# Layer 2 of a two-layer transformer kernel: GpSimd's powers, masks, gathers and folds in another order

## The chip, the cores and the metric

The kernel runs on one core of a Trainium2 chip. The metric is the device time of one execution in microseconds (us), and the time of a kernel is the median over several runs.

## The reference, cut to what matters

The program computes two layers on an input of 8 batches with 512 tokens of 128 features. Layer 1 is windowed attention plus a top-1 mixture of eight experts; it is not touched here. Layer 2 is causal attention with 16 heads of 64 (one key and one value head for all of them, normalised queries and keys) plus a gated feed-forward part. This is the core of layer 2 for one batch:

```python
xn = layernorm(x, g1)
q = xn @ Wq.T                          # 16 heads of 64
kv = xn @ Wkv.T                        # one k and one v, 64 wide
q, k = l2norm(q * 16), l2norm(k)       # each row divided by its length
sim = einsum('bhid,bjd->bhij', 4 * q, 4 * k)
sim = where(causal_mask, -max, sim)
attn = softmax(sim)
out = layernorm(einsum('bhij,bjd->bhid', attn, v) @ Wout.T, g2)
x = x + out + w_down(silu(gate) * up)
```

## The kernel before, in words

Five engines run programs of their own and meet at semaphores. Everything is written out by hand: the order of the lines in an engine's function is the order in which that engine issues them, and an instruction that waits holds up all that stands behind it on its engine.

Layer 2 (phase C, with the preparation of the next batch, R, woven into it) is a loop over the 8 batches. Seven of them run as a hardware loop with `last=False`, the eighth apart with `last=True`, without the work for a next batch. Within a batch, `attend` loops on every engine over n = 0 to 7. Each n is one **pair** of heads.

- TensorE (`pe`), at n: `scores(n)` in three parts ("thirds") into PSUM, `project_q(n + 2)`, `turn_q(n + 1)` (transposes), `gate_up` for small n, then `values1(n - 1)`, the product of masked probabilities and v. `project_q(n + 2)` needs the bank that `q_unit(n + 1)` on VectorE reads. `scores(n)` needs `q_lo` of pair n for its last matmuls.
- ScalarE (`act`), at n: the exponentials of the three thirds, the squares of the next projected q, and the copies of the turned q.
- VectorE (`dve`), at n: `q_sums` (sums of squares), `q_low(n + 1)`, `values_out(n - 1)` (the copy at L2056), then `q_unit(n + 2)`: `inverse` waits for GpSimd's power, clips it (TENSOR_SCALAR, L1958), takes the reciprocal (L1960), and L2011 scales the queries. At n = 3 it adds the experts' rows of the next batch, which GpSimd has gathered; at n = 4 it takes that batch's row statistics; at n = 5 and 6 it normalises and, in `add_blocks`, adds up the probability blocks of pairs 4 and 5.
- GpSimd (`pool`), at n: `q_length(n + 1)` raises the sums to the power 0.5 (TENSOR_TENSOR, L1272), four AFFINE_SELECTs mask pair n (L1313), and there are three rarer pieces. `fetch` issues indirect DMAs (L1231), one for each of four tiles, that gather the experts' rows of the next batch; `both_roots` computes two inverse roots for that batch's norms (L1098 to L1101); `fold(k)` issues an accumulating DMA (L1293, 384 KB) that adds the second key block's probabilities of pair k to those of the first. It is done for pairs 0 to 3 (`N_FOLD = 4`), and it waits until `values1(k)` has read them.

The folded blocks save TensorE matmuls in `sums1(m)`, which forms the softmax denominators of pairs 2m and 2m + 1. `sums1(0)` stands in TensorE's program at the end of n = 5, `sums1(1)` at n = 6 between `scores(6)` and `turn_q(7)`.

In the text, "the power k" is `q_length(s, k, b)`, and "the masks of n" are the four selects of pair n. The power k is issued at n = k - 1 and feeds `q_unit(k + 1)`, which TensorE awaits at `project_q(k + 2)`, or at `turn_q(7)` for k = 6.

Of the kernel before, what the change touches and what calls it, by code (L numbers as in the profile page):

```python
# [16 lines left out]
ALU = mybir.AluOpType  # L17
# [46 lines left out]
N_FOLD = 4  # L64
# [34 lines left out]
PER_C = dict(squared=6, q_full=6, q_free=6, o_full=7, o_free=7, l_full=1, l_free=1, s_full=15, s_free=15, m_full=8, m_free=8, w_full=11, w_free=11,  # L99
             e_full=10, e_free=9, own=17, var=1, veps=1, rstd=1,  # L100
             sums=6, lens=6, q_lo=8, h1=3, masked=24, pv=4, added4=6, g_free=2, inverted=1, fin=1, stored=16,
             folded=16 * N_FOLD)

CREDITED = dict(q_lo=1, q_free=1, o_free=1, l_free=1, s_free=1, m_free=1, w_free=1, e_free=1, g_free=1, sums=1, h1=1, r_free=1, added=1, stored=1, pv=1,
                xt_free=1, y_full=1, y_free=1, staged=2, out0=1, out1=1, out2=1, out3=1)
# [148 lines left out]
def two_layers(nc, x, wq, bq, wk, bk, wv, bv, wo, bo, w_router, w1, b1, w2, b2,  # L254
# [4 lines left out]
    with ExitStack() as ctx:  # L259
# [104 lines left out]
        def probs_of(n, j):  # L364

            at, many, step, skip = ((1536, 512, 512, 0), (512, 384, 512, 0), (0, 256, 256, 0), (512, 128, 512, 384))[j]
            return probs1[n % PB][:, at:at + 2 * step].rearrange("p (c t) -> p c t", c=2)[:, :, skip:skip + many]
# [100 lines left out]
        def apart(eng):  # L468

            eng.sem_inc(s_apart[0 if eng is nc.vector else 1], 1)  # L470
# [21 lines left out]
        def _(pe):  # L492
            pe.wait_ge(s_pool, N_IDENT)

            def mm(out, lhs, rhs, start=True, stop=True):
                return pe.matmul(out, lhs, rhs, start=start, stop=stop, skip_group_check=True)  # L496
# [188 lines left out]
            s = SB  # L685
# [103 lines left out]
            def attend(b, last):  # L789
                s = SC  # L790
# [65 lines left out]
                def p_of(n, c, j):  # L856
                    at, many = ((1536, 512), (512, 384), (0, 256), (896, 128))[j]
                    at += c * (256 if j == 2 else 512)
                    return probs1[n % PB][:, at:at + many]
# [10 lines left out]
                def sums1(m):  # L870

                    if m == 0:
                        pe.wait_ge(s["g_free"].sem, s["g_free"].at(b, 0))
                    if m < N_FOLD // 2:
                        pe.wait_ge(s["folded"].sem, s["folded"].at(b, 32 * (m + 1)))
                    if m == 2:
                        pe.wait_ge(s["added4"].sem, s["added4"].at(b, 6))
                    for j in ((0, 2, 3), (0, 2, 3), (0,), range(NT))[m]:
                        for h in range(HG):
                            ins = mm(gather[32 * h:32 * h + 32, j * P:T], pick_sum[:, m, :], p_of(2 * m + h // 2, h % 2, j),  # L880
                                     start=(m == 0 and j == 0), stop=(m == NP // 2 - 1 and j == NT - 1))
                    ins.then_inc(s["pv"].sem, s["pv"].add(1))
# [177 lines left out]
        def _(pool):  # L1060
# [32 lines left out]
            def both_roots(b):  # L1093

                s = SR
                pool.wait_ge(s["var"].sem, s["var"].at(b, 1))
                apart(pool)
                pool.tensor_scalar(veps2[:, 0, :], mv[:, :, 1], EPS, None, ALU.add).then_inc(s["veps"].sem, s["veps"].add(1))  # L1098
                pool.tensor_scalar(veps2[:, 1, :], mv[:, :, 1], 1.0 + EPS, EPS * EPS, ALU.mult, ALU.add).then_inc(s["veps"].sem, s["veps"].add(1))
                pool.wait_ge(s["veps"].sem, s["veps"].at(b, 2))  # L1100
                pool.tensor_tensor(rstd2[:].rearrange("p a i -> p (a i)"), veps2[:].rearrange("p a i -> p (a i)"),  # L1101
                                   exponents[:, 0:2 * NT], ALU.pow).then_inc(s["rstd"].sem, s["rstd"].add(1))
# [27 lines left out]
            def attend(b):  # L1130

                for n in range(FINISH if now.kind == "finish" else SLOTS):
                    if n % HG == MASK_LAG % HG and (now.own if n >= MASK_LAG else now.past):
                        mask((n - MASK_LAG) % SLOTS // HG)
                    if n == AT_ADD_BIAS and now.own:
                        if now.kind == "first":
                            pool.wait_ge(s_early, 32)
                        add_bias(b)
                    if n == AT_ROOT and now.own and now.ahead:
                        x_root()  # L1140
# [31 lines left out]
            assert n_late[0] == N_LATE  # L1172
            now.open("first", 0)
            attend(0)
            for b in range(1, B - 1):
                now.open("loop", b)
                attend(b)
# [37 lines left out]
            def fetch_slots(b, behind=True):  # L1215

                s = SR
                s["picked"].restart()
                s["back"].restart()
                if behind:  # L1220
                    pool.wait_ge(s["added"].sem, s["added"].at(b, 0))
                apart(pool)
                pool.tensor_copy(slots_now[:], slots[:, bass.ds(b * NT, NT)]).then_inc(s["picked"].sem, s["picked"].add(1))

            def fetch(b, tiles_of):

                s = SR
                pool.wait_ge(s["picked"].sem, s["picked"].at(b, 1))
                apart(pool)
                for i in tiles_of:  # L1230
                    pool.indirect_dma_start(y_back[:, i, :], None, slots_y[0:(TT + NE - 1) * P], bass.IndirectOffsetOnAxis(  # L1231
                        ap=slots_now[:, i:i + 1], axis=0)).then_inc(s["back"].sem, s["back"].add(16))
# [35 lines left out]
            def q_length(s, k, b):  # L1268

                pool.wait_ge(s["sums"].sem, s["sums"].at(b, k))  # L1270
                half = half_of(s, k - 1 if s is SR else k)
                pool.tensor_tensor(q_len[:, half], q_sum[:, half], exponents[:, 2 * NT:4 * NT],  # L1272
                                   ALU.pow).then_inc(s["lens"].sem, s["lens"].add(1))

            def k_length(b):
                s = SR
                pool.wait_ge(s["sums"].sem, s["sums"].at(b, 1))
                pool.tensor_tensor(klen[:], ksum[:], exponents[:, 2 * NT:3 * NT], ALU.pow).then_inc(s["lens"].sem, s["lens"].add(1))

            def attend(b, last):  # L1280
                s = SC
                for name in ("veps", "rstd", "lens", "masked"):
                    s[name].restart()
                for name in () if last else ("veps", "rstd", "lens"):
                    SR[name].restart()

                def fold(n):

                    pool.wait_ge(s["o_full"].sem, s["O"].filled(b, ("o", n)))
                    if n:  # L1290
                        pool.wait_ge(s["folded"].sem, s["folded"].at(b, 16 * n))
                    apart(pool)
                    pool.dma_start(probs_of(n, 0)[:, :, P:T], probs_of(n, 1),  # L1293
                                   accum_op=ALU.add).then_inc(s["folded"].sem, s["folded"].add(16))

                s["folded"].restart()
                for n in range(NP):
                    if 0 <= n - 2 < N_FOLD:
                        fold(n - 2)
                    if n + 2 < NP:  # L1300
                        q_length(s, n + 1, b)
                    p = probs1[n % PB]
                    for third in (0, 1, 2):
                        ring = (s["M"], s["S"], s["W"])[third]
                        pool.wait_ge(ring.free.sem, ring.emptied(b, ("probs", n, third)))
                        apart(pool)
                        if third == 0:
                            diagonals = [p[:, 512:1536].rearrange("p (c t) -> p c t", c=2)[:, :, at:at + P] for at in (0, 384)]
                        else:
                            at, many = (None, (0, 512), (1536, 1024))[third]  # L1310
                            diagonals = [p[:, at:at + many].rearrange("p (c t) -> p c t", c=2)[:, :, 0:P]]
                        for v in diagonals:
                            ins = pool.affine_select(out=v, in_=v, compare_op=ALU.is_ge, fill=0.0, base=0,  # L1313
                                                     pattern=[[0, 2], [1, P]], channel_multiplier=-1)
                        ins.then_inc(s["masked"].sem, s["masked"].add(1))
                    if not last and n == 0:
                        fetch_slots(b + 1)
                    if not last and n in (1, 2):
                        fetch(b + 1, (2 * n - 2, 2 * n - 1))
                    if not last and n == 4:  # L1320
                        both_roots(b + 1)
                if not last:
                    k_length(b + 1)
                    q_length(SR, 2, b + 1)
                    q_length(SR, 3, b + 1)
                root(s, 1, b)
# [878 lines left out]
```

## Time and profile before

| | |
|---|---|
| time, median of 3 runs | 1240.59 us (1240.56 to 1241.66) |
| the profiled execution's own time | 1239.02 us |
| its span, first to last instruction | 1237.2 us |
| layer 2 in it | from about 610 us on; 77.0 us for a batch |
| TensorE matmuls busy | 1145.6 us, 93% of the span |
| VectorE busy | 921.7 us, 74% |
| GpSimd busy | 490.6 us, 40% |

The shares are means over the whole program. Within layer 2 the seven batches of the loop look nearly the same, so the rows below are mostly of one of them, whose n = 0 begins at about 1005 us.

### The profile page before, as it was taken

The numbers are of one execution on the slowest core, as the hardware profiler recorded it, in microseconds if no ns is written. First come the engines' busy times: TensorE is split into PE (matmuls) and PEld (weight loads), VectorE is DVE, ScalarE is ACT, GpSimd is POOL, SyncE is SP. The second block draws the span as 40 slices with busy tenths as digits, with TensorE's granted clock in tenths as the row PEclk, the third lists the DMA queues.
The fourth block names the chain that finished last, engine by engine and source line by source line (L and its number), as shares of the span: only waits on it lengthen the run. The fifth ranks groups of instructions, "written<-read, shape, count | busy, mean of one in ns | idle before, by whom it ended". The sixth has DMA issues, their size and how long they took to land.

```text
span 1237.2 us, 26393 instructions
## 1 busy us (share of the span) xinstructions
PE 1145.6 (93%) x8475; PEld 782.4 (63%) x8475; DVE 921.7 (74%) x2473; ACT 672.3 (54%) x1290; POOL 490.6 (40%) x691
## 2 busy tenths in 40 slices
PE   5999999999999998899399999999999999999996
PEld 3656666666666554799265857657576575765764
DVE  7888888888888897455456868668686686866755
ACT  2767676666676755355173552735527355273550
POOL 5122212121222311554364481744817448274450
PEclk8999999999999998899799999999999999999999
DMA  3311212020101000122011030210302103021020
GB/s 89 101 44 48 56 28 57 26 60 26 33 18 27 18 18 1 44 64 55 15 35 27 9 59 0 42 25 8 59 0 42 25 8 59 0 49 19 15 46 10
DMA packets 43718, 42.31 MB, mean 34 GB/s; under 512 B 7040, under 2 KB 36224, under 8 KB 43648
## 3 DMA queue, kind: packets, MB, share of 16 engines
q0 software_dynamic: 11008, 17.31, 8.0%
q1 hardware_dynamic: 32640, 24.15, 7.3%
q8 instruction: 34, 0.56, 0.2%
q14 instruction: 36, 0.29, 0.1%
HBM read 13.72 MB, written 6.75 MB: 17 GB/s over the span
## 4 chain that ended last, share of the span: by engine, by line
issue 19%; PE 11%; POOL 9%; DVE 7%; DMA 3%; ACT 1%; POOLq 0%; DVEq 0%; ACTq 0%
PE pair L496 4%; POOL q_len L1272 3%; DMA arena<-arena 3%; PE gather L496 2%; PE ring_d L496 2%; POOL arena L1231 2%; POOL arena L1313 2%; PE ring_a L496 1%; PE pair L500 1%; DVE q_len L1958 1%; DVE stats L1574 1%; POOL arena L1293 1%; DVE arena L2106 1%; DVE q_rn L1960 1%; ACT arena L1515 1%
## 5 line engine op out<-in xcount | busy, mean ns | idle before, releaser
L1378 ACT ACTIVATE arena<-ring_a 128x384 f32<-128x384 f32 (+1 forms) x512 | 253.6, 550 | 147.1 <-PE ring_a L496 146.9
L1126 POOL TENSOR_SCALAR_AFFINE_SELECT arena<-arena 128x512 f32<-128x512 f32 x128 | 82.4, 643 | 366.6 <-ACT arena L1378 366.4
L496 PE MATMUL ring_a<-q_max,rows 128*128 128x384 f32 (+1 forms) x512 | 197.2, 388 | 2.2 <-DVE q_max L1684 1.8
L1670 DVE CUSTOM_DVE_ANT_0 arena<-pair,arena 128x384 bf16<-128x384 f32 (+1 forms) x269 | 161.3, 614 | 23.6 <-PE pair L496 19.1
L1272 POOL TENSOR_TENSOR q_len<-q_sum,exponents 128x8 f32<-128x8 f32 x64 | 113.6, 1775 | 85.1 <-DVE q_sum L2000 85.1
L1535 ACT ACTIVATE arena<-ring_a 128x1024 f32<-128x1024 f32 x96 | 99.1, 1032 | 75.9 <-PE ring_a L496 75.7
L496 PE MATMUL ring_a<-q_parts,k_rows 64*128 64x384 f32 (+2 forms) x1152 | 128.3, 344 | 3.4 <-ACT q_parts L1523 2.4
L496 PE MATMUL ring_a<-arena,v_aug 128*32 128x384 f32 (+1 forms) x1024 | 123.5, 553 | 1.7 <-POOL arena L1126 0.6
L496 PE MATMUL pair<-arena,v_aug 128*64 128x512 f32 (+3 forms) x768 | 114.0, 439 | 3.4 <-ACT arena L1535 3.0
L496 PE MATMUL pair<-rows,q_rows 128*128 128x384 f32 (+1 forms) x269 | 110.0, 411 | 3.3 <-DMA rows<-k_rows 2.5
L496 PEld LDWEIGHTS ring_a<-q_max,rows 128*128 128x128 f32 x512 | 96.8, 191 | 21.4 <-ACT arena L1378 5.3
L496 PEld LDWEIGHTS ring_a<-q_parts,k_rows 64*128 64x128 f32 x1152 | 90.0, 187 | 23.7 <-issue 12.6
L1313 POOL TENSOR_SCALAR_AFFINE_SELECT arena<-arena 128x256 f32<-128x256 f32 x192 | 80.9, 531 | 45.5 <-ACT arena L1535 43.9
L496 PEld LDWEIGHTS pair<-arena,v_aug 128*64 128x64 f32 x768 | 51.1, 136 | 71.9 <-issue 58.7
L1670 DVE CUSTOM_DVE_ANT_0 arena<-gather,arena 128x512 bf16<-128x512 f32 (+1 forms) x124 | 78.2, 630 | 17.6 <-PE gather L496 11.4
L496 PEld LDWEIGHTS pair<-rows,q_rows 128*128 128x128 f32 x269 | 51.2, 191 | 57.4 <-DVE mx L1670 34.9
L2056 DVE COPY arena<-pair 128x512 f32<-128x512 f32 x64 | 44.2, 691 | 52.3 <-PE pair L496 51.8
L1670 DVE CUSTOM_DVE_ANT_0 arena<-ring_d,arena 128x384 bf16<-128x384 f32 (+1 forms) x119 | 73.2, 615 | 9.8 <-PE ring_d L496 6.5
L2000 DVE TENSOR_REDUCE q_sum<-arena 128x8 f32<-128x512 f32 x64 | 43.8, 684 | 44.6 <-ACT arena L1507 44.6
L496 PE MATMUL ring_d<-wq_sb,o_raw 128*128 128x128 f32 x384 | 55.6, 288 | 18.0 <-DVE o_n L2011 9.9
L496 PEld LDWEIGHTS ring_d<-wq_sb,o_raw 128*128 128x128 f32 x384 | 46.5, 191 | 37.5 <-DVE q_nat_sb L2011 18.3
L1440 ACT ACTIVATE arena<-ring_a,arena 128x128 f32<-128x128 f32 x156 | 43.6, 377 | 47.3 <-PE ring_a L496 46.9
(275 smaller groups left out, 2380.9 us busy)
## 6 DMA issues: line engine op xcount, KB each, us to landing
arena<-arena POOLq DMA_DIRECT2D x32, 384.0 KB, 4.6
rows<-k_rows SPq DMA_DIRECT2D x128, 64.0 KB, 2.0
arena<-in_w SPq DMA_DIRECT2D x16, 256.0 KB, 2.8
slots_y<-arena SPq DMA_DIRECT2D x39, 64.0 KB
x_all<-in_x SPq DMA_DIRECT2D x8, 256.0 KB, 3.8
tokens_x<-xn SPq DMA_DIRECT2D x8, 256.0 KB, 2.7
out<-o_t SPq DMA_DIRECT2D x8, 256.0 KB, 2.3
arena<-tokens_x,tokens_now POOLq DMA_INDIRECT x40
```

Of the source, the lines that this page charges most:

```text
L496: return pe.matmul(out, lhs, rhs, start=start, stop=stop, skip_group_check=True)
L500: return [pe.transpose(slot[:, i * P:(i + 1) * P], tile_of(i), ident[:]) for i in range(n)][-1]
L1126: pool.affine_select(out=v, in_=v, compare_op=ALU.is_ge, fill=0.0, base=0, pattern=[[0, HG], [1 if late else -1, P]], channel_multiplier=- ...
L1231: pool.indirect_dma_start(y_back[:, i, :], None, slots_y[0:(TT + NE - 1) * P], bass.IndirectOffsetOnAxis(ap=slots_now[:, i:i + 1], axis=0) ...
L1272: pool.tensor_tensor(q_len[:, half], q_sum[:, half], exponents[:, 2 * NT:4 * NT], ALU.pow).then_inc(s["lens"].sem, s["lens"].add(1))
L1313: ins = pool.affine_select(out=v, in_=v, compare_op=ALU.is_ge, fill=0.0, base=0, pattern=[[0, 2], [1, P]], channel_multiplier=-1)
L1378: act.activation(probs[:, t % NT, h, 0:many], A.slot(("cols", c))[:, 0:many], ACT.Exp).then_inc(A.free.sem, A.free.add(1))
L1440: ins = act.activation(hidden[:, u % 2, c], hidden_bank(u, c), ACT.Relu, bias=staged[:, u, AT_B1 + c:AT_B1 + c + 1])
L1535: act.activation(dst, src, ACT.Exp).then_inc(ring.free.sem, ring.free.add(1))
L1670: dve.tensor_tensor_reduce(dump[:, h % 2, 0:many], M.slot(("max", n))[:, 0:many], masks[:, m, at:at + many], 1.0, LOWEST, ALU.add, ALU.max ...
L2000: dve.reduce_sum(q_sum[:, half_of(s, k)], q_sq, AX.X).then_inc(s["sums"].sem, s["sums"].add(1))
L2056: dve.tensor_copy(o1[:, n, :], ring.slot(("o", n))[:]).then_inc(ring.free.sem, ring.free.add(1))
```

## The change

On GpSimd alone the order is changed: in each n the power comes first, then the masks, then the gathers, then the folds. The four gathers are issued as one, two, one at n = 0, 1, 2 (before: two at n = 1, two at n = 2). Fold 0 moves from the start of n = 2 to its end, fold 1 from the start of n = 3 to its end, fold 2 from the start of n = 4 to its end, and fold 3 from the start of n = 5 to the end of n = 4, ahead of `both_roots`. The semaphore `folded`, on which each fold waited for the one before it, becomes two: `folded0` for pairs 0 and 1, `folded1` for pairs 2 and 3. No fold waits for another any more.

```diff
-             folded=16 * N_FOLD)
+             folded0=32, folded1=32)
...
                     if m < N_FOLD // 2:
-                        pe.wait_ge(s["folded"].sem, s["folded"].at(b, 32 * (m + 1)))
+                        pe.wait_ge(s[f"folded{m}"].sem, s[f"folded{m}"].at(b, 32))
...
                     pool.wait_ge(s["o_full"].sem, s["O"].filled(b, ("o", n)))
-                    if n:
-                        pool.wait_ge(s["folded"].sem, s["folded"].at(b, 16 * n))
+                    folded = s[f"folded{n // 2}"]
                     apart(pool)
                     pool.dma_start(probs_of(n, 0)[:, :, P:T], probs_of(n, 1),
-                                   accum_op=ALU.add).then_inc(s["folded"].sem, s["folded"].add(16))
-
-                s["folded"].restart()
+                                   accum_op=ALU.add).then_inc(folded.sem, folded.add(16))
+
+                for name in ("folded0", "folded1"):
+                    s[name].restart()
                 for n in range(NP):
-                    if 0 <= n - 2 < N_FOLD:
-                        fold(n - 2)
                     if n + 2 < NP:
                         q_length(s, n + 1, b)
...
-                    if not last and n in (1, 2):
-                        fetch(b + 1, (2 * n - 2, 2 * n - 1))
+                    if not last and n < 3:
+                        fetch(b + 1, ((0,), (1, 2), (3,))[n])
+                    for of in {2: (0,), 3: (1,), 4: (2, 3)}.get(n, ()):
+                        fold(of)
                     if not last and n == 4:
                         both_roots(b + 1)
```

First place: GpSimd's program from the masks of n = 2 to the power 4 of n = 3 in the loop over batches, before the change. `arena<-slots_y` is a gather, `arena<-arena 128x2x384` a fold.

```order
L1313 AFFINE_SELECT arena<-arena 128x2x128
L1231 DMA arena<-slots_y,slots_now 128x128 x2
L1289 REGISTER_ALU
L1291 ISA
L1293 DMA arena<-arena 128x2x384
L1270 REGISTER_ALU
L1272 TENSOR_TENSOR q_len<-q_sum,exponents 128x8
```

The same place of the changed kernel:

```order
L1311 AFFINE_SELECT arena<-arena 128x2x128
L1231 DMA arena<-slots_y,slots_now 128x128
L1289 ISA
L1292 DMA arena<-arena 128x2x384
L1270 REGISTER_ALU
L1272 TENSOR_TENSOR q_len<-q_sum,exponents 128x8
```

Ahead of the power 4 stand now one gather and fold 0, where there were two gathers and fold 1.

Second place: GpSimd's program from the last mask of n = 4 to the power 6 of n = 5, before. `veps` and `rstd` are `both_roots`.

```order
L1313 AFFINE_SELECT late<-late 128x2x128
L1098 TENSOR_SCALAR veps<-mv 128x4
L1099 TENSOR_SCALAR veps<-mv 128x4
L1100 ISA
L1101 TENSOR_TENSOR rstd<-veps,exponents 128x8
L1289 REGISTER_ALU
L1291 REGISTER_ALU
L1293 DMA arena<-arena 128x2x384
L1270 REGISTER_ALU
L1272 TENSOR_TENSOR q_len<-q_sum,exponents 128x8
```

The same place of the changed kernel:

```order
L1311 AFFINE_SELECT late<-late 128x2x128
L1289 REGISTER_ALU
L1292 DMA arena<-arena 128x2x384
L1289 REGISTER_ALU
L1292 DMA arena<-arena 128x2x384
L1098 TENSOR_SCALAR veps<-mv 128x4
L1099 TENSOR_SCALAR veps<-mv 128x4
L1100 ISA
L1101 TENSOR_TENSOR rstd<-veps,exponents 128x8
L1270 REGISTER_ALU
L1272 TENSOR_TENSOR q_len<-q_sum,exponents 128x8
```

Folds 2 and 3 stand now back to back between the masks and `both_roots`, and no fold stands between `both_roots` and the power 6.

## Rows read from the trace of the kernel before

**Rows 1.** One batch: us, then busy us of PE, PEld, DVE, ACT, POOL

```profile
1001.00:1078.00 77.00, 72.95 (x637) 51.62 (x636) 55.75 (x116) 38.27 (x59) 41.55 (x56) 1.00 0.15 27
```

**Rows 2.** Waits from 605 to 1143 us: us in total, times, longest

```profile
DVE q_len L1958 <- POOL q_len L1272: 30.7, 34, 2.0
...
PE ring_d L496 <- DVE o_n L2011: 9.9, 7, 1.5
...
PE ring_d L496 <- DVE q_nat_sb L2011: 6.8, 14, 1.1
...
PE gather L496 <- DMA arena<-arena: 4.0, 7, 1.0
```

**Rows 3.** Timeline of PE: start, duration, work, [idle before it, releaser]

```profile
1031.66 0.86 PE L496 MATMUL ring_a<-q_parts,k_rows 64*128 64x512 f32 x6
1034.02 1.16 PE L496 MATMUL ring_d<-wq_sb,o_raw 128*128 128x128 f32 x8 [1.50 <-DVE o_n L2011]
...
1046.76 0.87 PE L496 MATMUL ring_a<-q_parts,k_rows 64*128 64x512 f32 x6
1048.04 1.72 PE L496 MATMUL gather<-arena,pick_sum 128*32 128x512 f32 x24 [0.41 <-DMA arena<-arena]
1049.68 0.66 PE L500 MATMUL pair<-ident,o_n 128*128 128x128 f32 x4
...
1052.57 1.08 PE L496 MATMUL ring_a<-q_parts,k_rows 64*128 64x384 f32 x12
```

**Rows 4.** Timeline of POOL, n = 1 to 5, and one row of the last batch

```profile
1015.85 1.64 POOL L1272 TENSOR_TENSOR q_len<-q_sum,exponents 128x8 f32<-128x8 f32 x1 [2.01 <-DVE q_sum L2000]
...
1023.30 1.68 POOL L1272 TENSOR_TENSOR q_len<-q_sum,exponents 128x8 f32<-128x8 f32 x1 [0.37 <-DVE q_sum L2000]
...
1026.63 1.39 POOL L1231 DMA_INDIRECT arena<-slots_y,slots_now  x1 [0.18 <-issue]
1028.31 0.98 POOL L1231 DMA_INDIRECT arena<-slots_y,slots_now  x1 [0.30 <-issue]
1029.26 1.42 POOL L1293 DMA_DIRECT2D arena<-arena  x1
1030.10 2.30 POOL L1272 TENSOR_TENSOR q_len<-q_sum,exponents 128x8 f32<-128x8 f32 x1
...
1034.46 1.24 POOL L1293 DMA_DIRECT2D arena<-arena  x1 [0.60 <-DMA arena<-arena]
1036.62 1.67 POOL L1272 TENSOR_TENSOR q_len<-q_sum,exponents 128x8 f32<-128x8 f32 x1 [0.92 <-DVE q_sum L2000]
1038.27 1.49 POOL L1313 TENSOR_SCALAR_AFFINE_SELECT late<-late 128x256 f32<-128x256 f32 x4
1041.30 0.24 POOL L1098 TENSOR_SCALAR veps<-mv 128x4 f32<-128x4 f32 x1 [1.55 <-DVE mv L1583]
...
1043.53 1.26 POOL L1293 DMA_DIRECT2D arena<-arena  x1
1044.37 2.12 POOL L1272 TENSOR_TENSOR q_len<-q_sum,exponents 128x8 f32<-128x8 f32 x1
...
1188.54 1.66 POOL L1272 TENSOR_TENSOR q_len<-q_sum,exponents 128x8 f32<-128x8 f32 x1 [1.77 <-DVE q_sum L2000]
```

**Rows 5.** Timeline of DVE: n = 3, n = 6, and n = 2 of the seventh batch

```profile
1030.45 0.69 DVE L2056 COPY arena<-pair 128x512 f32<-128x512 f32 x1 [0.43 <-PE pair L496]
1032.43 0.48 DVE L1958 TENSOR_SCALAR q_len<-q_len 128x8 f32<-128x8 f32 x1 [1.28 <-POOL q_len L1272]
...
1051.57 0.69 DVE L2019 TENSOR_TENSOR q_parts<-arena,q_parts 128x512 fp32r<-128x512 f32 x1
...
1101.39 1.44 DVE L1958 TENSOR_SCALAR q_len<-q_len 128x8 f32<-128x8 f32 x1
```

**Rows 6.** DMA from 1043 to 1049 us: GB/s in 40 slices; an issue to landing

```profile
GB/s 0 0 0 0 0 0 0 0 0 0 0 0 0 0 0 51 195 184 184 184 164 215 195 174 195 174 174 184 195 143 11 0 0 0 0 0 0 0 0 0
...
arena<-arena POOLq DMA_DIRECT2D x1, 384.0 KB, 4.5
```

## The prediction

> **What bounds the kernel now.** I first read the busy time batch by batch. In a batch of layer 2 TensorE's matmuls are busy for 72.95 of 77.0 us, while VectorE has 55.75 and GpSimd 41.55 [rows 1]. So GpSimd's sum of work bounds nothing. Its order matters only where TensorE stands still for it, and at most about 4 us a batch are there to be had.
>
> The table of waits says where [rows 2]. In the seven batches of the loop TensorE waits before `project_q` 9.9 us on `o_n` and 6.8 us on `q_nat_sb`, the two buffers of scaled queries, and 4.0 us before `sums1(1)` on a fold's DMA. VectorE in turn waits 34 times, 30.7 us in all, for GpSimd's power. The timelines show which of these the order on GpSimd makes.
>
> Place A is `project_q(6)` at n = 4. `scores(4)` ends at 1032.52 (1031.66 + 0.86), and `project_q(6)` starts at 1034.02 after 1.50 us idle [rows 3]. It waited for `q_unit(5)`, whose first instruction started at 1032.43 after VectorE had stood idle for 1.28 us [rows 5], waiting for the power 4. That power ends at 1032.40. Its row starts inside the row of fold 1, but a power alone takes 1.64 us, so it really began at about 1030.76, when the fold's issue was over (1029.26 + 1.42). Ahead of it stood two gathers, from 1026.63, and fold 1 [rows 4].
>
> Place B is `sums1(1)` at n = 6. `scores(6)` ends at 1047.63, and `sums1(1)` starts at 1048.04 [rows 3], because fold 3 was issued only at 1043.53, behind `both_roots` [rows 4], and a fold takes 4.5 us from issue to landing [rows 6].
>
> **The change, part by part.** I work on this batch; the other six of the loop stand alike.
>
> Gather moved to n = 0: 0. After the masks of n = 0 GpSimd is idle for 2.01 us before the power 2 [rows 4], and a gather costs at most 1.68 us (the larger step from one gather to the next row, 1026.63 to 1028.31). If that cover were gone, it would cost what sticks out. The two gathers at n = 1 stand where two stood.
>
> Fold 0 leaves the start of n = 2: 0. The power 3 was idle for 0.37 us until VectorE's sum was there [rows 4], so the fold hid under that wait.
>
> Place A: the power 4 now has one gather and one fold ahead of it instead of two gathers and one fold. The saving is one gather. Its price is bounded by the two steps in the rows, 1.68 us (first to second gather) and 0.95 us (second gather to fold, 1028.31 to 1029.26). I take 0.95, because the row it replaces is the one in front of the fold. The power 4 then ends at 1031.45, `project_q(6)` starts at 1033.07, and 0.55 us of the idle time stays. From below the price is not zero, since a gather is removed; from above it can't give more than the 1.50 us of idle time. Sum A: 7 x 0.95 = 6.65 us, between 7 x 0.35 (a stall described under the rivals) and 7 x 1.50 = 10.5.
>
> Fold 1 at the end of n = 3: 0. The power 5 behind it was idle for 0.92 us waiting for VectorE, after a fold that had itself waited 0.60 us for the landing of the one before (gone with the shared semaphore) and taken 1.24 [rows 4]. One fold stood there before and one stands there now.
>
> Place B: everything from place A on comes 0.95 us earlier. The power 5 starts at 35.67 (I drop the thousand), the masks of n = 4 end at 38.8 (1.65 + 1.49 later), fold 2 is issued at 38.8 and fold 3 at about 40.0, one issue of 1.24 us later. While a fold moves its data the queue is full at about 184 GB/s [rows 6], which is 2.15 us for 384 KB. So fold 3 lands 2.15 us behind fold 2, which lands at 38.8 + 4.5 = 43.3: at 45.4. `sums1(1)` can begin at 47.63 - 0.95 = 46.68. It no longer waits, with a margin of 1.2 us, and the whole 4.0 us [rows 2] are saved, not more, since nothing else is removed there.
>
> `both_roots` now comes behind two folds. It starts at 41.3 instead of 41.30, so it loses nothing in absolute time, and lasts 2.23 us (1041.30 to 1043.53) [rows 4]. Its reader on VectorE stands behind `q_unit(7)`. The power 6 follows at once, without the fold between (1.26 us), and ends at 45.2 instead of 46.49. Who waits for it: `turn_q(7)`, formerly at 49.68 and now at 48.3, and through `add_blocks(4)` also `q_low(7)`, which ended at 52.26 (1051.57 + 0.69) [rows 5], 5.77 us after the power. It is needed 8 matmuls of 12 into the first third of `scores(7)`, that is 0.7 us after 52.57 [rows 3]. So the power 6 might have ended 1.0 us later before, at 47.5; with the batch 1.36 us earlier the limit is 46.1. The new 45.2 keeps to it with 0.9 us, and that is the cover of this edit.
>
> The last batch: 0. It has no gathers and no `both_roots`, and its powers wait 1.77 us for VectorE [rows 4].
>
> **Sum.** 6.65 + 4.0 = 10.65 us. On the profiled execution: span 1237.2 to 1226.6, its own time 1239.02 to 1228.4. The median of the runs stands 1.57 us above that execution: 1240.59 - 10.65 = 1229.9 us. A change under 0.2% (2.5 us) could not be told from none.
>
> **The rivals.**
>
> R1, a stall takes back most of A. VectorE ends the copy of `values_out(2)` at 1031.14 [rows 5]. If the power ends just before that and not after it, GpSimd's four selects are already running when the first instruction of `q_unit` comes. In the seventh batch that TENSOR_SCALAR, started at 1101.39 with no idle time before it, took 1.44 us instead of 0.48 [rows 5]. The power 4 would have to come 1.26 us earlier than now: too much for my 0.95, within reach of 1.68. `q_unit(5)` would then run from 31.14 for 1.44, against 32.43 for 0.48, so place A would gain 1032.91 - 1032.58, about 0.35 us. Sum 7 x 0.35 + 4.0 = 6.5 us: 1234.1.
> The Trainium skill ("SBUF — State Buffer", section "Who interferes with whom") says that VectorE's 2-port modes, which a `tensor_scalar` can enter, and GpSimd's instructions exclude each other over a shared port pair, and that the second to issue blocks until the first finishes. By that rule the wait is one select, a quarter of the 1.49 us of four, and A would keep at least 0.95; the 0.48 agrees with it, the 1.44 doesn't.
>
> R2, GpSimd can't issue fold 3 while fold 2 is under way. No row shows two folds in flight: each waited for its forerunner. If GpSimd were held until fold 2 lands, at 43.3, fold 3's issue would end at 44.5, `both_roots` at 46.8, the power 6 at 48.4 and `q_low(7)` at 54.2, 0.9 us after the moment (53.3) at which `scores(7)` needed it before. That is 7 x 0.9 = 6 us slower: 1246.6. The point that decides is the end of the power 6 at 47.5, that is, a hold of more than 2.3 us. For it speaks only that it was never shown; against it that fold 1 was issued 0.95 us behind a gather, with no gap [rows 4].
>
> R3, both folds are issued but move slower together, so that place B keeps its wait and A alone is left: 6.65 us, 1233.9. This needs fold 3 to land more than 1.2 us late.
>
> R4, place A gains its whole 1.50 us, the gather costing 1.68 and no stall arising: 10.5 + 4.0 = 14.5 us, 1226.1.
>
> R5, what is gained at A and B is given back later in the batch (a wait moves from `project_q(6)` to another input that is hardly earlier, such as the squares on ScalarE), and the time stays near 1240. Against it: in n = 5 and in the tail of the batch TensorE's inputs all follow from TensorE itself.
>
> **How the numbers follow.** My forecast 0.46 (own range 1228 to 1232), R1 0.20, R3 0.08, R4 0.09, R5 0.08, R2 0.09. Faster by over 0.2% is the sum of the first four, 0.83, no change 0.08, slower 0.09. The range takes in R4 at its low end and R1 and R3 at its high end, with 1 to 2 us for the unread starts of two issues: 1225.5 to 1235.5, which leaves out the 0.17 of R5 and R2.
>
> **What would show it.** In each batch of the loop: idle time before `project_q(6)` near 0.55 instead of 1.50; none before `sums1(1)`; folds 2 and 3 issued about 1.3 us apart, each issue near 1.24 us; fold 3 landing 2 us or so behind fold 2; the power 6 ending about 1.3 us earlier than before against the start of the batch; no new wait before `project_q(4)`, `turn_q(7)` or `scores(7)`. A period of 75.5 us a batch instead of 77.0. A TENSOR_SCALAR of over 1 us in `q_unit(5)` means R1; a gap between the folds' issues means R2.

## The result and the profile after

The changed kernel takes 1231.89 us (median of 5 runs, 1227.2 to 1234.95), the one before 1241.66 us (5 runs beside it, 1240.56 to 1245.0). The ratio is 0.9917 with a 95% interval of 0.9894 to 0.9939: faster by 0.8%, about 10 us. The forecast was 1229.9 us, in a range from 1225.5 to 1235.5.

The chain is read batch by batch. The table of waits from 605 to 1143 us of the changed kernel (releaser, us in total, times, longest) has for the rows of [rows 2]:

```profile
DVE q_len L1958 <- POOL q_len L1272: 20.7, 35, 1.3
...
PE ring_d L496 <- DVE o_n L2011: 6.2, 7, 0.9
...
PE ring_d L496 <- DVE q_nat_sb L2011: 6.0, 14, 0.6
```

The wait of TensorE's matmuls for a fold's DMA, 4.0 us before, is gone from it. The wait on `o_n` fell from 9.9 to 6.2 us only. These are places B and A. TensorE's timeline shows them in the sixth batch (start, duration, work, [idle before, releaser]); the rows answer to [rows 3]:

```profile
1028.12 0.86 PE L496 MATMUL ring_a<-q_parts,k_rows 64*128 64x512 f32 x6
1029.86 1.16 PE L496 MATMUL ring_d<-wq_sb,o_raw 128*128 128x128 f32 x8 [0.88 <-DVE o_n L2011]
...
1042.81 0.86 PE L496 MATMUL ring_a<-q_parts,k_rows 64*128 64x512 f32 x6
1043.60 1.72 PE L496 MATMUL gather<-arena,pick_sum 128*32 128x512 f32 x24
1045.25 0.66 PE L500 MATMUL pair<-ident,o_n 128*128 128x128 f32 x4
```

`project_q(6)` has 0.88 us idle in front of it instead of 1.50, `sums1(1)` at 1043.60 none instead of 0.41. GpSimd's timeline in the same batch, against [rows 4]:

```profile
1012.30 1.67 POOL L1272 TENSOR_TENSOR q_len<-q_sum,exponents 128x8 f32<-128x8 f32 x1 [0.27 <-DVE q_sum L2000]
...
1019.78 1.67 POOL L1272 TENSOR_TENSOR q_len<-q_sum,exponents 128x8 f32<-128x8 f32 x1 [1.84 <-DVE q_sum L2000]
...
1023.09 1.32 POOL L1231 DMA_INDIRECT arena<-slots_y,slots_now  x1 [0.18 <-issue]
1024.42 1.39 POOL L1292 DMA_DIRECT2D arena<-arena  x1
1025.56 2.42 POOL L1272 TENSOR_TENSOR q_len<-q_sum,exponents 128x8 f32<-128x8 f32 x1
1027.20 2.21 POOL L1311 TENSOR_SCALAR_AFFINE_SELECT arena<-arena 128x256 f32<-128x256 f32 x4
...
1035.55 2.43 POOL L1292 DMA_DIRECT2D arena<-arena  x2
1037.48 0.80 POOL L1098 TENSOR_SCALAR veps<-mv 128x4 f32<-128x4 f32 x1
...
1040.29 1.63 POOL L1272 TENSOR_TENSOR q_len<-q_sum,exponents 128x8 f32<-128x8 f32 x1
```

The moved gather is hidden: the power 2 still waits 0.27 us for VectorE, though the gather itself first waited 0.86 us for the row numbers in `slots_now`. From the gather of n = 2 to the end of the power 4 it is 1027.98 - 1023.09 = 4.89 us, before it was 1032.40 - 1026.63 = 5.77. The removed gather was worth 0.88 us on GpSimd (0.95 was forecast). But TensorE got 0.62. VectorE's timeline, against [rows 5], shows where the rest went:

```profile
1026.91 0.69 DVE L2056 COPY arena<-pair 128x512 f32<-128x512 f32 x1 [0.43 <-PE pair L496]
1028.02 0.73 DVE L1958 TENSOR_SCALAR q_len<-q_len 128x8 f32<-128x8 f32 x1 [0.41 <-POOL q_len L1272]
1028.78 0.20 DVE L1960 RECIPROCAL q_rn<-q_len 128x8 f32<-128x8 f32 x1
```

The small TENSOR_SCALAR behind the power takes 0.73 us in all seven batches, where it took 0.48 in six of seven.

Folds 2 and 3 were issued back to back in 2.43 us. The power 6 behind them ended at 1041.92, which is 1.0 us earlier than before against the `project_q(2)` of its batch (1.3 was forecast). The DMA view of 1036 to 1040 us (GB/s in 40 slices; an issue and its median us to landing) shows that both were under way at once and followed each other at full rate, against [rows 6]:

```profile
GB/s 0 0 0 0 0 0 0 0 0 0 0 0 0 154 200 169 169 169 184 184 169 184 200 184 184 169 215 169 184 169 200 184 200 154 138 16 123 184 215 184
...
arena<-arena POOLq DMA_DIRECT2D x2, 384.0 KB, 5.2
```

The profiled execution itself is only 4.07 us faster than that of before (1234.95 against 1239.02), less than the medians. From the first `gate_up(0)` of the second batch to that of the last, six batches took 461.90 us (695.57 to 1157.47) and take 455.14 (696.64 to 1151.78): 1.13 us a batch, about the 0.62 at A and some 0.5 at B (forecast: 1.5). With the first batch (79.19 to 78.05) the loop gained 7.9 us. Outside it this execution lost 3.8: 2.2 us ahead of the loop, and 1.6 behind its end, where the changed code has no part. A clock row tells of the latter (busy us of PE, PEld, DVE, ACT, POOL, then the granted clock):

```profile
1213.80:1219.00 5.20, 4.92 (x21) 4.25 (x22) 3.09 (x5) 0.00 (x0) 0.00 (x0) 0.67 0.00 0
```

After 1.91 us idle the granted clock of TensorE was 0.67 on the mean of this stretch, that is, partly at 1.2 GHz, and eight matmuls there took 2.03 us where they took 1.16 us before, after 1.90 us idle. So executions differ by some us in such places. The ratio over all runs, not the pair of profiles, is the result; of its 10 us the traces show these 7.9.

### The profile page after: what moved, and what is told of

The parts are those of the page before. It is cut to its first block and busy times, and to the rows that moved or that the text cites. A ratio compares the mean times of both kernels' runs of the same rounds, so it can differ in the third digit from the quotient of the medians.

```text
span 1233.1 us, 26372 instructions
## 1 busy us (share of the span) xinstructions
PE 1149.3 (93%) x8475; PEld 785.1 (64%) x8475; DVE 921.1 (75%) x2473; ACT 672.3 (55%) x1290; POOL 494.6 (40%) x691
## 5 line engine op out<-in xcount | busy, mean ns | idle before, releaser
L1272 POOL TENSOR_TENSOR q_len<-q_sum,exponents 128x8 f32<-128x8 f32 x64 | 111.1, 1736 | 88.3 <-DVE q_sum L2000 88.1
L1535 ACT ACTIVATE arena<-ring_a 128x1024 f32<-128x1024 f32 x96 | 99.1, 1032 | 75.4 <-PE ring_a L496 75.4
L1311 POOL TENSOR_SCALAR_AFFINE_SELECT arena<-arena 128x256 f32<-128x256 f32 x192 | 83.6, 545 | 42.2 <-ACT arena L1535 41.4
L2056 DVE COPY arena<-pair 128x512 f32<-128x512 f32 x64 | 44.2, 691 | 53.7 <-PE pair L496 53.7
L496 PEld LDWEIGHTS gather<-wout_sb,arena 128*128 128x128 f32 x512 | 66.7, 196 | 2.6 <-DVE arena L2106 0.6
```

Source lines behind the costliest of these rows:

```text
L1535: act.activation(dst, src, ACT.Exp).then_inc(ring.free.sem, ring.free.add(1))
L2056: dve.tensor_copy(o1[:, n, :], ring.slot(("o", n))[:]).then_inc(ring.free.sem, ring.free.add(1))
```

## The experiments

All ratios below are to the kernel before on the same chip. The chips differ (its median was 1245.41, 1231.35, 1230.83 and 1242.33 us in the four sessions), so times are compared by ratio. The 95% intervals reach 0.2 to 0.35% to either side. In the rows of a kernel with added lines, L1958, L2011 and L2056 carry line numbers higher by two or four.

**Gathers alone, folds alone, folds chained, and a fold ahead of the masks** ran in one session. The first, from the kernel before:

```diff
-                    if not last and n in (1, 2):
-                        fetch(b + 1, (2 * n - 2, 2 * n - 1))
+                    if not last and n < 3:
+                        fetch(b + 1, ((0,), (1, 2), (3,))[n])
```

> The kernel before with only the gathers moved (one, two, one at n = 0, 1, 2); folds, their places and their one semaphore as before. Theory: the time of the change is two separate terms. This one has term A alone: one gather less ahead of the power 4, the idle time before project_q(6) 1.50 -> about 0.9, the wait of sums1(1) stays near 0.5. 7 x 0.6 = 4.4 us faster than before: about 1236. Rival: the gain at A came from the folds (fold 0 there instead of fold 1, which waited for a semaphore): then no gain, 1240 to 1241.

Measured 1238.27 us, ratio 0.9936 (0.991 to 0.9962). TensorE's timeline:

```profile
880.78 1.16 PE L496 MATMUL ring_d<-wq_sb,o_raw 128*128 128x128 f32 x8 [0.90 <-DVE o_n L2011]
...
895.07 1.72 PE L496 MATMUL gather<-arena,pick_sum 128*32 128x512 f32 x24 [0.52 <-DMA arena<-arena]
```

Term A is the gather's alone and is there without the folds; the wait at B stays. A batch lasts 76.5 us in this trace, about 0.5 less than before, which comes near the expected 4 us; the ratio says 8 us, with an interval from 5 to 11.

The second is the changed kernel with the gathers at two and two again:

```diff
-                    if not last and n < 3:
-                        fetch(b + 1, ((0,), (1, 2), (3,))[n])
+                    if not last and n in (1, 2):
+                        fetch(b + 1, (2 * n - 2, 2 * n - 1))
```

> The changed kernel with the gathers back at two and two (n = 1, 2); folds and semaphores as changed. Theory: term B alone. Ahead of the power 4 stand two gathers and fold 0, as many as before, so the idle time before project_q(6) stays at 1.50; the wait before sums1(1) goes: 4.0 us faster than before, about 1237. Rival: with place A late by what it was, other waits take B's gain too and the time is that of before. The two terms together should be the whole change (about 1.1 us a batch).

Measured 1250.79 us, ratio 1.0041 (1.0016 to 1.0066): slower than before. The expectation fell. VectorE's timeline has the cause:

```profile
882.92 1.09 DVE L1958 TENSOR_SCALAR q_len<-q_len 128x8 f32<-128x8 f32 x1 [1.20 <-POOL q_len L1272]
```

TensorE's timeline and its clock by stretches have the consequence:

```profile
885.12 1.83 PE L496 MATMUL ring_d<-wq_sb,o_raw 128*128 128x128 f32 x8 [2.02 <-DVE o_n L2011]
886.74 1.06 PE L500 MATMUL pair<-ident,o_n 128*128 128x128 f32 x4
887.73 2.90 PE L496 MATMUL pair<-arena,v_aug 128*64 128x512 f32 x16
```

```profile
884.00:885.00 1.00, 0.00 (x0) 0.00 (x0) 0.84 (x4) 0.46 (x1) 1.00 (x2) 1.00 0.00 0
885.00:886.00 1.00, 0.88 (x5) 0.88 (x6) 0.85 (x3) 0.00 (x0) 0.55 (x1) 0.71 0.00 0
886.00:887.00 1.00, 1.00 (x7) 1.00 (x7) 0.50 (x1) 0.01 (x1) 0.00 (x0) 0.50 1.00 164
```

The power ended as late as before (VectorE waited 1.20 us for it, 1.28 before), but the TENSOR_SCALAR took 1.09 us instead of 0.48, in all seven batches. Why it took longer here with the same wait ahead of it stays open. The idle time grew from 1.50 to 2.02 us, and behind it the granted clock fell to 0.50, which is 1.2 GHz: `project_q` took 1.83 instead of 1.16 us, the transposes 1.06 instead of 0.60, `values1` 2.90 instead of 2.38. B did gain (there is no idle time before `sums1(1)`), and yet a batch became 1.4 us longer (78.4 against 77.0). So the two halves of the change don't add up: folds alone cost 0.4%, gathers alone give 0.6%, together they give 0.8% (the last measured in another session).

The third has the changed kernel's places and semaphores, and every fold waits for the one before it:

```diff
                     folded = s[f"folded{n // 2}"]
+                    if n:
+                        pool.wait_ge(s[f"folded{(n - 1) // 2}"].sem, s[f"folded{(n - 1) // 2}"].at(b, 16 + 16 * ((n - 1) % 2)))
```

> The changed kernel with every fold waiting again for the landing of the fold before it (places and semaphores as changed). Theory: this is the hold that my second rival of the prediction spoke of. Fold 3 waits some 4.5 us for fold 2, both_roots and the power 6 stand behind it and end some 4 us later; q_low(7) comes 2.3 us too late for scores(7), so a batch gets about 2 us longer: 14 to 16 us slower than the changed kernel, 5 us slower than before. Rival: only the landing of fold 3 counts (44.6 instead of 42 against sums1(1) at 43.6): 7 us slower than the changed kernel, as fast as before or a little faster.

Measured 1253.57 us, ratio 1.0067 (1.0041 to 1.0093), against 0.9917 of the changed kernel. That is 1.5% or 19 us, a little over the theory and far from the rival. A batch lasts 78.6 us against 75.85, which over seven batches is the same 19 us. TensorE's timeline shows the theory's waits, the last ones on `q_low(7)`:

```profile
902.62 1.72 PE L496 MATMUL gather<-arena,pick_sum 128*32 128x512 f32 x24 [1.55 <-DMA arena<-arena]
904.90 0.65 PE L500 MATMUL pair<-ident,o_n 128*128 128x128 f32 x4 [0.57 <-DVE o_n L2013]
909.00 0.50 PE L496 MATMUL ring_a<-q_parts,k_rows 64*128 64x384 f32 x4 [0.43 <-DVE q_parts L2021]
```

The early fold 3 is thus worth something only because it doesn't wait for fold 2.

The fourth issues fold 1 between the power 4 and the masks of n = 3:

```diff
                         q_length(s, n + 1, b)
+                    if n == 3:
+                        fold(1)
...
-                    for of in {2: (0,), 3: (1,), 4: (2, 3)}.get(n, ()):
+                    for of in {2: (0,), 4: (2, 3)}.get(n, ()):
```

> The changed kernel with fold 1 issued between the power 4 and the masks of n = 3 instead of behind them. Theory: the TENSOR_SCALAR L1958 behind the power 4 takes 0.73 us (0.16 where nothing disturbs it) because GpSimd's selects start at the same moment; with the fold's issue in their place it takes about 0.16 to 0.2, and the idle time before project_q(6) goes from 0.88 to about 0.3: 7 x 0.55 = 3.9 us faster than the changed kernel, about 1228. Rival: the 0.73 comes from the transfer of fold 0, which is under way then: it stays 0.73 and the time stays.

Measured 1234.74 us, ratio 0.9906 (0.9873 to 0.994), not to be told from the changed kernel. TensorE's and GpSimd's timelines:

```profile
957.38 1.16 PE L496 MATMUL ring_d<-wq_sb,o_raw 128*128 128x128 f32 x8 [0.58 <-DVE o_n L2013]
...
959.52 2.38 PE L496 MATMUL pair<-arena,v_aug 128*64 128x512 f32 x16 [0.54 <-POOL arena L1313]
```

```profile
955.02 2.01 POOL L1292 DMA_DIRECT2D arena<-arena  x1
955.84 3.62 POOL L1313 TENSOR_SCALAR_AFFINE_SELECT arena<-arena 128x256 f32<-128x256 f32 x4
```

VectorE's timeline:

```profile
955.85 0.42 DVE L1960 TENSOR_SCALAR q_len<-q_len 128x8 f32<-128x8 f32 x1 [0.42 <-POOL q_len L1272]
```

L1958 (L1960 there) fell to 0.42 us in this batch and three others, and the idle time to 0.58, so the selects do take part in it. They are not the whole of it: the selects began only when the fold's issue was over, so no select ran during these 0.42 us, and yet it is more than the 0.16 us that L1958 takes alone. GpSimd was issuing fold 1 at that moment; whether that makes the other 0.26 us, no run separates. And the masks came so late that `values1(3)` waited 0.54 us for them. They took 2.4 us from the end of the fold's issue (957.03) to 959.46 instead of 1.49, while VectorE ran its additions at n = 3. The Trainium skill ("SBUF — State Buffer", section "Who interferes with whom") says that a VectorE instruction with two SBUF inputs contends with a GpSimd instruction that reads SBUF; that fits, but no run here separates it.

**Who makes the TENSOR_SCALAR slow?** The second session ran on another chip, with the changed kernel itself as yardstick.

> The changed kernel unaltered, on the same chip as the runs beside it, as their yardstick: 0.992 of the time of before, with 0.88 us idle before project_q(6) in each batch and none before sums1(1).

Measured 1220.18 us, ratio 0.991 (0.9875 to 0.9944), as in the result above. The trace, however, is another one at place A: the power 4 ends before VectorE's copy. GpSimd's and VectorE's timelines:

```profile
936.08 1.78 POOL L1272 TENSOR_TENSOR q_len<-q_sum,exponents 128x8 f32<-128x8 f32 x1
937.72 1.58 POOL L1311 TENSOR_SCALAR_AFFINE_SELECT arena<-arena 128x256 f32<-128x256 f32 x4
```

```profile
937.30 0.69 DVE L2056 COPY arena<-pair 128x512 f32<-128x512 f32 x1 [0.32 <-PE pair L496]
937.91 1.43 DVE L1958 TENSOR_SCALAR q_len<-q_len 128x8 f32<-128x8 f32 x1
939.37 0.20 DVE L1960 RECIPROCAL q_rn<-q_len 128x8 f32<-128x8 f32 x1
```

L1958 took 1.43 us and ended with the last of the four selects (939.30), and 1.07 us idle time stood before `project_q(6)`. This is the stall of rival R1, in six of the seven batches. The seventh had none (L1958 0.28 us) and lasted 74.25 us instead of 75.6. In return `project_q(5)` had lost its wait of 0.3 us, since ScalarE read a projected q sooner; why ScalarE wakes sooner in some batches, as in the seventh of the kernel before, I did not find.

Beside it fold 0 stood ahead of the power 3 again, as in the kernel before:

```diff
                 for n in range(NP):
+                    if n == 2:
+                        fold(0)
                     if n + 2 < NP:
                         q_length(s, n + 1, b)
...
-                    for of in {2: (0,), 3: (1,), 4: (2, 3)}.get(n, ()):
+                    for of in {3: (1,), 4: (2, 3)}.get(n, ()):
```

> The changed kernel with fold 0 issued at the start of n = 2 again, ahead of the power 3, where it hides under a wait; ahead of the power 4 stands one gather alone. The power 4 can then start as soon as VectorE's sum is there and ends some 0.8 us earlier, 0.4 us before VectorE's copy ends. Theory (rival R1 of the prediction): the four selects already run when L1958 comes, it loses to up to all of them (steps of 0.36 us: 0.38, 0.73, 1.09, 1.44), so the idle time before project_q(6) shrinks by 0 to 0.3 us only: 0 to 2 us faster than the changed kernel. Rival: GpSimd's lateness alone set that wait: L1958 takes 0.2 us, the whole 0.88 goes, 6 us faster.

Measured 1223.62 us, ratio 0.9919 (0.9888 to 0.995), no gain over the changed kernel. Place A was all but free (0.15 us idle or none), but the stall had moved to n = 2, where neither the theory nor the rival had it. GpSimd's, VectorE's and TensorE's timelines there:

```profile
937.12 1.54 POOL L1313 TENSOR_SCALAR_AFFINE_SELECT arena<-arena 128x256 f32<-128x256 f32 x4
```

```profile
937.32 1.38 DVE L1960 TENSOR_SCALAR q_len<-q_len 128x8 f32<-128x8 f32 x1
```

```profile
939.80 1.16 PE L496 MATMUL ring_d<-wq_sb,o_raw 128*128 128x128 f32 x8 [1.02 <-DVE q_nat_sb L2013]
```

L1958 of n = 2 took 1.38 us, and `project_q(5)` waited 1.02 us.

Now the direct test: the changed kernel, in which the masks of n = 3 wait until L1958 is done.

```diff
                         q_length(s, n + 1, b)
+                    if n in (3,):
+                        pool.wait_ge(s["own"].sem, s["own"].at(b, 3 * n + 1))
```

> The changed kernel with one wait more: at n = 3 the masks wait until VectorE's L1958 behind the power 4 is done. Nothing else moves; fold 0's transfer is under way as before. Theory: L1958 takes 0.16 us instead of 0.73 because no select competes; idle before project_q(6) 0.88 -> about 0.3: 3.9 us faster than the changed kernel. Rival: the 0.73 is the DMA's traffic or the wake-up: it stays, and the masks merely come later: no change or slightly slower.

Measured 1214.31 us, ratio 0.9858 (0.9825 to 0.9891): 0.5% or 6 us faster than the changed kernel beside it. The two intervals overlap a little, but five of the six executions were faster than every one of the changed kernel. VectorE's and TensorE's timelines:

```profile
933.29 0.69 DVE L2058 COPY arena<-pair 128x512 f32<-128x512 f32 x1 [0.32 <-PE pair L496]
933.89 0.16 DVE L1960 TENSOR_SCALAR q_len<-q_len 128x8 f32<-128x8 f32 x1
```

```profile
934.49 0.86 PE L496 MATMUL ring_a<-q_parts,k_rows 64*128 64x512 f32 x6
935.29 1.16 PE L496 MATMUL ring_d<-wq_sb,o_raw 128*128 128x128 f32 x8
```

The fold's data moved from about 932.7 to 934.8 us by the DMA view, so its transfer was under way as before; L1958 took 0.16 or 0.17 us in all seven batches, and TensorE had no idle time before `project_q(6)`. The selects made the stall, not the DMA's transfer. The same 0.16 or 0.17 us at n = 3 shows in every batch of the five other runs below that hold these masks. A batch lasts 74.2 us (906.92 to 981.14).

The last kernel of the second session joined the wait at n = 0, 2 and 3 with fold 0 ahead of the power 3:

```diff
+                    if n in (0, 2, 3):
+                        pool.wait_ge(s["own"].sem, s["own"].at(b, 3 * n + 1))
```

> Fold 0 ahead of the power 3 as in the run with it alone, and the masks of n = 0, 2 and 3 wait for VectorE's L1958. Theory: the power 4 is there when VectorE's copy ends, L1958 takes 0.16 to 0.2 us each time; idle before project_q(6) 0.88 -> 0 to 0.1, before project_q(5) 0.32 -> 0.1, before project_q(3) 0.54 -> 0.35: 1.2 us a batch, 8 us faster than the changed kernel, about 0.985 of before. Rival: the held masks come too late for values1 and a new wait on GpSimd's selects takes the gain: as the changed kernel or slower.

Measured 1218.1 us, ratio 0.9885 (0.9858 to 0.9913), short of the single wait. L1958 took 0.17 us at n = 0, 2 and 3, but `project_q(5)` waited 1.13 us. Ahead of the power 3 stood now the held masks of n = 0, two gathers and fold 0, and it ended 22.2 us after the batch's first `gate_up(0)` instead of 21.0 with fold 0 alone. Fold 0 in its old place is free only while VectorE's sum is late.

**Where else the wait pays.** Two more sessions. The wait at n = 0 and 3 (`if n in (0, 3)`):

> The changed kernel with the masks of n = 0 and of n = 3 waiting for VectorE's L1958 (the run before had the wait at n = 3 alone, 0.986 of before). Theory: L1958 at n = 0 takes 0.17 instead of 0.36, the idle time before project_q(3) goes from 0.54 to 0.36: 0.18 x 7 = 1.3 us faster than with one wait, about 0.985 of before. Rival: the masks of n = 0 and the gather behind them push the power 2 and make VectorE late at n = 1: same as with one wait or slower.

Measured 1220.26 us, ratio 0.9914 (0.9886 to 0.9943). The 0.54 us before `project_q(3)` became 0.36 as expected, but the stall showed up at n = 2 in five of the seven batches: L1958 1.37 us, `project_q(5)` 1.01 us idle. Here fold 0 was in its new place, so the stall there is not fold 0's alone: the held masks of n = 0 make the power 3 late too. The wait alone, in the kernel before:

> The kernel before, unchanged but for the wait of the masks at n = 3 for VectorE's L1958. Theory: L1958 goes from 0.48 to 0.16, the idle time before project_q(6) from 1.50 to about 1.2, 0.3 x 7 = 2.2 us faster than before (0.998), since there the selects took one step of 0.36 only; the wait is worth more after the change, where they took two to four. Rival: the wait holds back fold 2 and the power 5 and gives nothing.

Measured 1234.88 us, ratio 1.002 (0.9999 to 1.004): no gain. L1958 of n = 3 was 0.17 us, but in most batches of its trace L1958 of n = 2 took 1.44 us (`project_q(5)` 1.09 us idle), and at n = 4 it took 0.74 (`project_q(7)` 0.70 us idle). There is no trace of the kernel before on this chip, so it isn't known which of these stalls it has there without the wait. The single wait in the changed kernel, once more:

> The changed kernel with the wait at n = 3 once more, beside the two runs of this call: 0.986 of before, L1958 at n = 3 0.16 us, no idle time before project_q(6).

Measured 1217.2 us, ratio 0.9874 (0.9851 to 0.9897). In three of the seven batches L1958 of n = 4 took about 1.3 us and `project_q(7)` waited 0.95 us. So the last run let the masks of n = 3 and 4 wait:

> The changed kernel with the masks of n = 3 and of n = 4 waiting for VectorE's L1958. With the wait at n = 3 alone some batches lose again 0.96 us before project_q(7), where L1958 of n = 4 meets the four selects and takes 1.31 us. Theory: with both waits L1958 takes 0.16 to 0.3 at n = 3 and 4 in every batch, no idle time before project_q(6) and project_q(7); 0.985 to 0.987 of before and less spread. Rival: the held masks of n = 4 push folds 2 and 3, both_roots and the power 6, so sums1(1) or scores(7) wait: slower than with one wait.

Measured 1232.21 us, ratio 0.9912 (0.9891 to 0.9934). The stalls at n = 3 and 4 were gone (0.17 and 0.16 us), but ScalarE was in its later timing here, with 0.3 us idle before each of `project_q(5)` and `project_q(6)`. The rival has a share too: the power 6 came later (VectorE waited 2.75 us for it, 2.17 with the single wait), and `scores(7)` started slowly, its first third 1.41 us instead of 1.08 with 0.19 us idle behind it. A batch lasts 75.4 us, against 74.2 with the single wait. This was another session, and its interval hardly overlaps those of the single wait (0.9851 to 0.9897 and 0.9825 to 0.9891); which of the two is better in the same timing stays open. The best version that was measured twice is the changed kernel with the one wait at n = 3: 0.986 and 0.987 of before.

## Why the prediction was right

**The sum.** -10.65 us was forecast for the median, -9.8 measured (ratio 0.9917, 10 us). That is close partly by luck. The traces of the loop show 7.9 us, 4.3 at A and 3.6 at B, against 6.65 + 4.0; the 2 us between 7.9 and the measured change lie within the ratio's interval (7.6 to 13 us).

**Place B: right, in place and size.** "`sums1(1)` can begin at 47.63 - 0.95 = 46.68. It no longer waits": it doesn't, in any batch. By the DMA view of the changed kernel fold 3's last bytes moved at about 1041.8, 1.8 us before `sums1(1)` began; a fold's landing came some 0.4 us after its last bytes before the change, so the margin was about 1.4 us, an estimate, where I had 1.2. In the rows the power 6 ends 3.3 us before `turn_q(7)` starts (1041.92, 1045.25). The chained folds showed what B rests on, and R2's mechanism with it: hold fold 3 until fold 2 has landed, and the whole is 19 us slower than the change. The price that I gave R2 in the prediction, 6 us over the kernel before, came out as 0.67% or 8 us, with a wait of `sums1(1)` for fold 3's landing (1.55 us) that R2 had left out. R2 did not happen in the change itself, because two folds can be in flight.

**Place A: right in cause, mis-sized.** The step "Sum A: 7 x 0.95 = 6.65 us" took a microsecond of GpSimd for one of TensorE. GpSimd's part was right (0.88 measured); between them stands L1958, for which I had left 0.48 us and which took 0.73: two of the selects passed ahead of it (they ended at about 1028.3 and 1028.7) instead of one. TensorE gained 0.62, so A was 4.3 us and not 6.65.

**R1 was given 0.20 and a threshold that is too simple.** I wrote that L1958 stalls if the power ends before VectorE's copy and is at 0.48 us otherwise. The runs show a loss in steps of a select: 0.38, 0.73, 1.09 and 1.44 us, 0.35 us apart where a select takes 0.37, for one to four of them. It took 0.73 with the power ending 0.4 us after the copy, and 1.43 with it ending before. What decides how many pass is not shown: with the power 1.1 to 1.3 us after the copy it took 0.48 before and 1.09 with the folds alone, and in the run with the single wait it began at n = 2 only 0.17 us after the power's end, with that pair's masks behind it, and took 0.24. On the second chip R1's stall was there, and the ratio was still 0.991. The wait before `project_q(5)` had gone in return; that this is the reason is argued only, since the kernel before has no trace on that chip and can have had stalls of its own.
The rule of the Trainium skill that I had weighed there ("SBUF — State Buffer", section "Who interferes with whom": the second to issue waits until the first finishes) fits the first select only; measured is that the following selects of the group can get in ahead of the waiting instruction too. No run shows in which mode L1958 ran.

**Gather at n = 0 and fold 0 at n = 2: right in the change** (0.27 us of the cover left; the gather's 0.86 us wait for `slots_now` was not in my working, but it lies in the same idle time). That moving fold 0 away cost and gave nothing held in the profiled execution of the changed kernel, where the power 3 waits 1.84 us for VectorE; where VectorE's sum is early, its old place costs 1 us at `project_q(5)`, as one run shows with fold 0 alone and one with held masks beside it.

**R3, R4, R5** did not occur. What R4 described, no idle time before `project_q(6)`, came with the single wait: 74.2 us a batch, where the changed kernel beside it took 75.4 to 75.6 in the batches with the stall (the first batch apart, which is longer in both).

## What to carry to other kernels

A microsecond saved on the engine that comes late is passed on only through the small instruction that waits for it. Look at that instruction's own duration, not just at when it starts: if it varies in steps, another engine's burst may be let in ahead of it, and a wait that holds the burst back by a fraction of a microsecond can add to the reordering: here 0.5% on top of its 0.9%, and nothing in the kernel before. And undo halves one at a time: here one half alone is slower than before.

## What the runs showed of the hardware

- A TENSOR_SCALAR on 128x8 elements in SBUF, on VectorE, takes 0.16 us alone. When GpSimd runs four AFFINE_SELECTs (1.49 us together) at that moment, it takes 0.38, 0.73, 1.09 or 1.44 us in most cases: by these steps one to four selects (0.37 us each) pass first. A wait that keeps the selects off brings it back to 0.16 at that place, in every batch. Beside GpSimd's issue of a fold, with no select running, it took 0.42.
- With the folds alone TensorE was idle for 2.0 us in each of the seven batches, and within 2 us behind it the granted clock fell from 1.00 to 0.50 (2.4 to 1.2 GHz) and was back at 1.00 some 3 to 4 us later; the eight matmuls of `project_q(6)` took 1.56 to 2.08 us in six batches and their usual 1.16 in the seventh, where the clock fell just behind them. Idle for 1.50 us was followed by no fall before the change. After 1.91 us near the program's end the clock fell with the changed kernel, after 1.90 us in the same place before it did not.
- Two accumulating DMAs of 384 KB, issued 1.2 us apart, share the queues one after the other at about 184 GB/s. GpSimd is not held for the first (2.43 us for both issues, 1.24 to 1.42 for one).
